# A two-layer transformer block on one core: gate and up products interleaved in the first batch's FFN, and five score banks in the last plain group

## What is computed

```
x = x + attention(norm(x))          # 16 heads of 8, softmax
x = x + ffn(norm(x))                # rounded to FP4 in blocks of 16
x = x + rotary_attention(norm(x))   # causal, own projections
x = x + mixture_of_experts(norm(x)) # top 2 of 8
# ffn: h = silu(fq(x) @ fq(w_gate).T) * (fq(x) @ fq(w_up).T); out = fq(h) @ fq(w_down).T
```

## Time and profile before

| what | us |
|---|---|
| median of 3 runs | 1920.32 (1916.94 to 1920.45) |
| the profiled execution | 1912.49 |
| its span, first to last instruction | 1910.8 |
| busy: TensorE, ScalarE, VectorE, GpSimd | 1647.2, 1442.0, 1196.8, 269.1 |

### The profile page before, as it was taken

How to read it: one execution, slowest core, us unless ns; L and a number is a source line. 1 busy time by engine, 2 the same in 40 slices (tenths; PEclk the granted TensorE clock), 3 DMA queues, 4 the chain that set the end, 5 groups by cost and what they waited for, 6 DMA issues and landing times. The chain is left out here.

```text
span 1910.8 us, 33432 instructions
## 1 busy us (share of the span) xinstructions
PE 1647.2 (86%) x12948; PEld 631.4 (33%) x12948; DVE 1196.8 (63%) x2146; ACT 1442.0 (75%) x2508; POOL 269.1 (14%) x292
## 2 busy tenths in 40 slices
PE   5599999999999999854888898998889888883995
PEld 3122222222222222242334342433333333222674
DVE  7999999999999998577364536454545423223220
ACT  4187777787877778722998999999989999992221
POOL 4400000000000000022000100010001022312466
PEclk9699999999999999966999999999999999996998
DMA  5201111111111110003111221113102222231433
GB/s 170 94 26 49 39 43 38 38 43 38 38 38 44 38 38 22 7 25 111 55 50 59 73 86 50 51 58 108 47 32 73 79 88 95 99 118 47 133 57 30
DMA packets 69839, 115.85 MB, mean 61 GB/s; under 512 B 9689, under 2 KB 54597, under 8 KB 65072
## 3 DMA queue, kind: packets, MB, share of 16 engines
q1 hardware_dynamic: 58416, 92.87, 15.3%
q0 software_dynamic: 11264, 20.83, 4.0%
HBM read 71.49 MB, written 42.14 MB: 59 GB/s over the span
## 5 line engine op out<-in xcount | busy, mean ns | idle before, releaser
L750 ACT ACTIVATE rows_and_probs<-psS 128x512 f32<-128x512 f32 x1024 | 556.4, 596 | 179.3 <-PE psS L648 177.6
L772 DVE TENSOR_REDUCE max_of_halves<-psM 128x2 f32<-128x1024 f32 x512 | 617.7, 1222 | 44.7 <-PE psM L617 15.4
L1574 ACT ACTIVATE exps<-cpsS 128x1024 bf16<-128x1024 f32 x512 | 545.6, 1107 | 25.4 <-PE cpsS L1338 24.7
L1338 PE MATMUL cpsS<-rotary_stack 128*128 128x512 bf16 x1024 | 302.9, 386 | 70.6 <-ACT exps L1574 28.7
L668 PE MATMUL psO<-rows_and_probs,plain_v 128*9 128x256 f32 x4096 | 317.1, 382 | 4.9 <-issue 2.3
L1584 ACT ACTIVATE cprobs<-cpsS 128x1024 f32<-128x1024 f32 x256 | 281.2, 1098 | 21.7 <-PE cpsO L1371 18.9
L1318 PE MATMUL cpsS<-rotary_stack 128*128 128x512 bf16 (+3 forms) x768 | 193.7, 329 | 53.5 <-ACT exps L1574 36.4
L617 PE MATMUL psM<-plain_top 64*128 64x512 bf16 x1024 | 209.8, 391 | 24.4 <-DVE max_of_halves L772 24.1
L648 PE MATMUL psS<-plain_top 64*128 64x512 bf16 x1024 | 213.2, 388 | 6.5 <-issue 6.5
L648 PE MATMUL psS<-plain_rest 64*128 64x512 bf16 x1024 | 207.7, 378 | 0.0
L1371 PE MATMUL cpsO<-cprobs,rotary_v 128*9 128x512 f32 (+3 forms) x1536 | 153.7, 488 | 0.8 <-DVE rotary_sums L1908 0.8
(11 more groups left out here) (294 smaller groups left out, 1682.4 us busy)
## 6 DMA issues: line engine op xcount, KB each, us to landing
rotary_stack<-q_parts SPq DMA_DIRECT2D x48, 192.0 KB
rotary_stack<-k_parts SPq DMA_DIRECT2D x48, 192.0 KB
rotary_stack<-q_rot_parts SPq DMA_DIRECT2D x48, 192.0 KB
rotary_stack<-k_rot_parts SPq DMA_DIRECT2D x48, 192.0 KB
tokens_taken<-parts_and_sums POOLq DMA_DIRECT2D x32, 259.0 KB, 4.2
plain_top<-q_parts SPq DMA_DIRECT2D x64, 96.0 KB
plain_top<-k_parts SPq DMA_DIRECT2D x64, 96.0 KB
e_x<-tokens_taken SPq DMA_DIRECT2D x8, 518.0 KB, 9.3
```

What stands on the lines that cost most here:

```text
L750: act.activation(pr[n % SLOTS_P][:, h, :], psS[u % RING][:, :], ACT.Exp, scale=SCALE).then_inc(s_e, 1)
L772: dve.tensor_reduce(mh[g % 2][:, :, hh, t, kh:kh + 1].rearrange("p e o -> p (e o)"), psM[n % 2][:, :, :], AX.X, ALU.max).then_inc(s_r, 1)
L1338: ins = pe.matmul(to[:, kh, :], q[:, x, y_ * P:(y_ + 1) * P], k[:, x, kh * CH:(kh + 1) * CH], start=True, stop=True)
L1574: act.activation(ex[d % EX][:, :, :], psS[n % 3][:, :, :], ACT.Exp, scale=SCALE, accum_out=den[:, at:at + 1]).then_inc(s_e, 1)
```

## The change

In the plain phase the scores of group 15 go round over five banks, the three of `psS` and the pair of `psM` that `merge_turn(15)` will use at the end. `last_user(u)` names the unit whose exponential frees the bank. Units 3 and 4 of the group instead wait for VectorE to have read the last turn out of that pair.

In the late phase VectorE clears the corners first, in the order of banks 4, 5, 6, 0, 1, 2, 3, and `cpsO` last. TensorE begins with the gate weights after the first clear, then turns the up and down weights, each after its bank's clear. The projection weights become a task of their own, `wq`, behind the last up product, with a bank of the ring. ScalarE copies the gate and up weights first, the down weights ahead of the first tanh, and the projection weights at `wq`. TensorE waits for two copies before the first gates, for four before the up products and later gates, for twelve before the projections. A gate needs the up product of the tile before. By the planner's rule, which I worked through, the order becomes

```diff
@@ -600,6 +600,19 @@
+        LAST, spare = (G - 1) * UNITS, psM[use["merge", G - 1, 0] % 2]
+        last_banks = [psS[(LAST + i) % RING][:, :] for i in range(RING)] + [spare[:, i, :] for i in range(2)]
+        def score_bank(u):
+            return psS[u % RING][:, :] if u < LAST else last_banks[(u - LAST) % len(last_banks)]
+        def last_user(u):
+            if u >= LAST + len(last_banks):
+                return u - len(last_banks)
+            return u - RING if RING <= u < LAST + RING else None
@@ -642,10 +655,15 @@
                         u, h = u0 + n, HEADS[i + n]
-                        if part == 0 and u >= RING:
-                            pe.wait_ge(s_e, u - RING + 1)
+                        if part == 0:
+                            before = last_user(u)
+                            if before is None and u >= RING:
+                                pe.wait_ge(s_r, use["turn", G - 1, 0] + 1)
+                            elif before is not None:
+                                pe.wait_ge(s_e, before + 1)
                         rows, hh = rows_of(h // (HG // 2)), h % (HG // 2)
-                        ins = pe.matmul(psS[u % RING][:, :], k[rows, hh, j * P:(j + 1) * P],
+                        ins = pe.matmul(score_bank(u), k[rows, hh, j * P:(j + 1) * P],
                                         q[rows, hh, cq * CH:(cq + 1) * CH], start=(part == 0), stop=(part == 1),
@@ -747,7 +765,7 @@
                         act.wait_ge(s_s, u + 1)
-                        act.activation(pr[n % SLOTS_P][:, h, :], psS[u % RING][:, :], ACT.Exp,
+                        act.activation(pr[n % SLOTS_P][:, h, :], score_bank(u), ACT.Exp,
                                        scale=SCALE).then_inc(s_e, 1)
@@ -1018,7 +1036,7 @@
     for t in range(TB):
-        tasks.append((("g", n, t), "slot", 0.5, [("x", n, t // TC)], 0.0))
+        tasks.append((("g", n, t), "slot", 0.5, [("x", n, t // TC)] + ([("u", n, t - 1)] if t and n == 0 else []), 0.0))
     if n:
@@ -1031,9 +1049,11 @@
                 tasks.append((("round_h", n, t // 2), "vector", 7.0, [("u", n, t), ("u", n, t - 1)], 0.0))
+    if n == 0:
+        tasks.append((("wq", n), "slot", 2.0, [("u", n, TB - 1)], 0.0))
     for c in range(2):
         for t in range(c * TC, (c + 1) * TC):
-            tasks.append((("h", n, t), "slot", 0.55, [("round_h", n, t // 2), ("d", n, c - 1)], 0.0))
+            tasks.append((("h", n, t), "slot", 0.55, [("round_h", n, t // 2), ("d", n, c - 1)] + ([("u", n, TB - 1)] if n == 0 else []), 0.0))
         tasks.append((("d", n, c), "slot", 0.7, [("h", n, t) for t in range(c * TC, (c + 1) * TC)], 0.0))
@@ -1160,7 +1180,7 @@
-    SLOT_KINDS = ("x", "g", "u", "h", "d", "px", "a", "s", "v", "m", "fy", "fo", "rt", "l", "ps")
+    SLOT_KINDS = ("wq", "x", "g", "u", "h", "d", "px", "a", "s", "v", "m", "fy", "fo", "rt", "l", "ps")
     use, bank_of, earlier = {}, [], []
@@ -1175,7 +1195,7 @@
     for label, k in use.items():
-        act_keeps = label[1] == 0 and label[0] in ("x", "h", "px")
+        act_keeps = label[1] == 0 and label[0] in ("x", "h", "px", "wq")
         if act_keeps:
@@ -1259,7 +1279,7 @@
         block = c.enter_context(nc.Block())
-        KEPT = 12
+        UP_KEPT, DOWN_KEPT, KEPT = 2, 4, 12
         BLOCKS = 2 * I // QB
@@ -1375,6 +1395,8 @@
                     wait_kept(pe, ("h", n, cc * TC + i))
+                    if n == 0:
+                        pe.wait_ge(s_wk, DOWN_KEPT)
                     for j, (at, width) in enumerate(FC):
@@ -1400,8 +1422,14 @@
                         ins = pe.transpose(to[:, i * P:(i + 1) * P], rows, p.ident[:, :])
+                elif kind == "wq":
+                    pe.wait_ge(s_w, 16 * 5)
+                    for t in range(4):
+                        ins = pe.transpose(to[:, t * P:(t + 1) * P], raw[:, t, :], p.ident[:, :])
                 elif kind in ("g", "u"):
                     t = label[2]
+                    if n == 0:
+                        pe.wait_ge(s_wk, UP_KEPT if (kind, t) < ("g", TC) else DOWN_KEPT)
                     wait_kept(pe, ("x", n, t // TC))
@@ -1417,10 +1445,14 @@
                     wait_kept(pe, ("px", n, cc))
+                    if n == 0:
+                        pe.wait_ge(s_wk, KEPT)
                     ins = pe.matmul(to[:, :], w[:, k if kind == "a" else 3 + k, :], xt[:, cc * CH:(cc + 1) * CH],
...
                     wait_kept(pe, ("px", n, label[2]))
+                    if n == 0:
+                        pe.wait_ge(s_wk, KEPT)
                     for i in range(TC):
@@ -1451,21 +1483,21 @@
-            pe.wait_ge(s_oz, 1 + len(banks))
             pe.wait_ge(fw.s_wq, 2)
+            for k in range(2):
+                pe.wait_ge(s_oz, k + 1)
+                for j, (at, width) in enumerate(FC):
+                    ins = pe.transpose(banks[4 + k][:, at:at + width], fw.raw[0:width, 3 * k + j, :], p.ident[0:width, 0:width])
+                ins.then_inc(s_wt, 1)
             for j, (at, width) in enumerate(FC):
-                ins = pe.transpose(banks[1][0:width, j * P:(j + 1) * P], fw.rawd[:, at:at + width], p.ident[:, :])
+                pe.wait_ge(s_oz, 3)
+                ins = pe.transpose(banks[6][0:width, j * P:(j + 1) * P], fw.rawd[:, at:at + width], p.ident[:, :])
             ins.then_inc(s_wt, 1)
-            for k in range(2):
-                for j, (at, width) in enumerate(FC):
-                    ins = pe.transpose(banks[2 + k][:, at:at + width], fw.raw[0:width, 3 * k + j, :], p.ident[0:width, 0:width])
-                ins.then_inc(s_wt, 1)
-            pe.wait_ge(s_w, 16 * 5)
-            for t in range(4):
-                ins = pe.transpose(banks[4][:, t * P:(t + 1) * P], raw[:, t, :], p.ident[:, :])
-            ins.then_inc(s_wt, 1)
-            pe.wait_ge(s_wk, KEPT)
             for _, label in plans[0]:
+                if label[0] == "x":
+                    pe.wait_ge(s_oz, 4 + label[2])
+                elif label == ("g", 0, 0):
+                    pe.wait_ge(s_oz, len(banks) + 1)
                 fill(label)
@@ -1494,24 +1526,29 @@
             def keep_weights():
-                act.wait_ge(s_wt, 1)
-                act.activation(wd[:, 0:2, :], banks[1][:, 0:2 * P].rearrange("p (c d) -> p c d", c=2), ACT.Copy).then_inc(s_wk, 1)
+                for k in range(2):
+                    act.wait_ge(s_wt, k + 1)
+                    act.activation(wg[:, k, :], banks[4 + k][:, 0:I], ACT.Copy).then_inc(s_wk, 1)
+            def keep_down():
+                turned = banks[6]
+                act.wait_ge(s_wt, 3)
+                act.activation(wd[:, 0:2, :], turned[:, 0:2 * P].rearrange("p (c d) -> p c d", c=2), ACT.Copy).then_inc(s_wk, 1)
                 last = FC[2][1]
-                act.activation(wd[0:last, 2, :], banks[1][0:last, 2 * P:3 * P], ACT.Copy).then_inc(s_wk, 1)
+                act.activation(wd[0:last, 2, :], turned[0:last, 2 * P:3 * P], ACT.Copy).then_inc(s_wk, 1)
+            def keep_square(turned):
                 for k in range(2):
-                    act.wait_ge(s_wt, k + 2)
-                    act.activation(wg[:, k, :], banks[2 + k][:, 0:I], ACT.Copy).then_inc(s_wk, 1)
-                act.wait_ge(s_wt, 4)
-                for k in range(2):
-                    src = banks[4][:, k * D:(k + 1) * D]
+                    src = turned[:, k * D:(k + 1) * D]
                     act.activation(w[:, k, :].rearrange("p (a d h) -> p a d h", a=HG, d=DH),
...
                         act.activation(to[:, i, :, :, :], src[:, 1 - i, :, :, :], ACT.Copy).then_inc(s_wk, 1)
-                act.activation(w[:, 2, :], banks[4][:, 2 * D:3 * D], ACT.Copy).then_inc(s_wk, 1)
-                act.activation(wo[:, :], banks[4][:, 3 * D:4 * D], ACT.Copy).then_inc(s_wk, 1)
+                act.activation(w[:, 2, :], turned[:, 2 * D:3 * D], ACT.Copy).then_inc(s_wk, 1)
+                act.activation(wo[:, :], turned[:, 3 * D:4 * D], ACT.Copy).then_inc(s_wk, 1)
+                act.wait_ge(s_wk, KEPT)
@@ -1529,6 +1566,8 @@
                 elif kind == "g" and n == 0:
+                    if label[2] == 0:
+                        keep_down()
                     act.wait_ge(s_f, use[label] + 1)
@@ -1549,7 +1588,10 @@
                     act.wait_ge(s_f, use[label] + 1)
-                    if kind in ("x", "px"):
+                    if kind == "wq":
+                        keep_square(bank(label))
+                        act.sem_inc(s_ka, 1)
+                    elif kind in ("x", "px"):
                         cc = label[2]
@@ -1722,7 +1764,7 @@
                 elif half == 0:
-                    dve.wait_ge(s_wt, 4)
+                    wait_read(dve, ("wq", 0))
                 mine = slice(half * TC * HG, (half + 1) * TC * HG)
@@ -1907,10 +1949,9 @@
+            for to in banks[4:] + banks[:4]:
+                dve.memset(to[FC[2][1]:P, 2 * P:3 * P], 0.0).then_inc(s_oz, 1)
             dve.memset(psO[:, :], 0.0).then_inc(s_oz, 1)
-            for to in banks:
```

(1 more changed line is left out.)

## The result

| | before | after |
|---|---|---|
| median of 5 runs, us | 1917.0 (1915.71 to 1920.45) | 1903.76 (1901.3 to 1907.75) |
| ratio, 95% interval | | 0.9928 [0.9917, 0.9939] |
| span of the profiled execution | 1910.8 | 1900.5 |

The change is faster, by 13.2 us between the medians.

A forecast was written before the change was run, and what follows sets the result against it. It took a loop of exponentials, value sums and scores to bound the last plain group, VectorE the stage to 903, ScalarE the rotary phase. Gains 0.3 + 9.9 = 10.2 us from 1920.32 gave 1910.1 us, range 1904.5 to 1916.

The forecast's parts named there:

- Five banks: Last plain group: scores wait for the exponential five before, not three; 0.3 us gained, bounds 0 and 3.2.
- no link of it waits for a bank: Last plain group: the 2.38 us loop of exponentials, value sums and scores never waits for a bank, so it stays.
- Rival A: Last plain group: TensorE, no longer late, also shortens waits for each half's first scores, up to 3.2 us; 1907.2, chance 0.10.
- Start of TensorE: Head of the late phase: one small clear precedes TensorE instead of 1.60 us of clears, so it starts at 810.13.
- First scaling: Head of the late phase: VectorE's first scaling at 819.2 instead of 829.07, 9.9 us earlier (9.4 to 10.8).
- Rounds: Rounding: two gates more per round are free, 7.10 us against 7.11; three rounds change by 0 (-0.2 to +1.9).
- Rival B: Rounding: GpSimd holds the second gate, 1912.0, chance 0.07; or holds all four products, 1921.5, chance 0.04.
- Projection weights: Late phase: their transposes and ScalarE's copies, moved behind the last up product, cost 0; without cover 2.5 us.
- Rival E: Head: planner doesn't interleave as the diff says, or last weight load is still awaited in front; 1918.6, chance 0.03.
- Second down product: Behind the last rounding: unchanged, 0 taken; wholly full clock would give 1.35 us, wholly half would cost 0.9.
- rival C: Before 903: down product becomes the bound, or stores fall due in another order; half the gain, 1915, chance 0.06.
- rival D: Rotary phase: its 16 groups lose their rhythm and ScalarE stands longer; 1926 at 1 us a group, chance 0.05.

The follow-up runs named there:

- late_only: The changed kernel with three score banks in the last plain group, as before the change; 1906.48 us, ratio 0.9942 to the kernel before.
- four_banks: The changed kernel with four score banks in the last plain group instead of five; 1902.43 us (2 runs), ratio 0.9933 to the kernel before.
- again: The changed kernel, unedited, run once more on another chip; 1903.06 us, ratio 0.9937 to the kernel before.
- unedited_beside: The changed kernel, unedited, run once more beside two other versions on the same chip; 1903.44 us, ratio 0.9937 to the kernel before.
- projections_in_front: The changed kernel with projection weights turned ahead of the rows, down-weight copies in front and all twelve copies awaited; 1914.6 us, 0.9983 to the kernel before.
- gates_first: The changed kernel without a gate's need for the preceding up product, so eight gates come first; 1909.78 us, ratio 0.9951 to the kernel before.
- four_scores: The changed kernel, issuing all four scores of a half before the previous half's value sums in the last plain group; 1899.86 us, 0.9921 to the kernel before.
- plain_only: The kernel before with only the five score banks in the last plain group; 1917.99 us, ratio 0.9996 to the kernel before.

## Why the prediction was wrong, point by point

Three terms were too small: the banks by 0.5 us, the first scaling by 1.3, the second down product by 1.35. The sign, the order of the terms and the mechanism of the largest were right. In the profiled executions group and head gave 13.8 us against 10.2 in the sum; the three terms are 3.2 of the difference, and 0.5 lie in small ones behind them. Behind the second and the third term stands one omission: TensorE's clock was put at a value between its two levels where the execution was at the full one. Between the medians the change gave 13.2, so the sum was 3.0 us short, and it was taken from a median that was itself 3.3 us too high. Together these are the 6.3 us between 1910.1 and 1903.76.

- **The median it was taken from** (1920.32, three runs between 1916.94 and 1920.45). Two more runs brought it to 1917.0, and other chips gave 1918.39, 1914.39 and 1915.42. I had written that a median scatters by some 2 us; the three runs were 3.3 off. The profiled execution, at 1912.49, had pointed the other way, and the forecast gave it no weight.
- **Five banks: 0.3 taken, 0.83 measured.** The step that failed is "no link of it waits for a bank". One did, in front of the value sums. In the kernel before they start 0.31 us behind the start of the last second part in front of them, also where they have waited for exponentials: those at 791.55 stand 0.31 behind a second part of 791.25, and 0.10 behind the end of the exponential they wait for. That second part was late because its score had waited for a bank. In the changed kernel the waiting sums of 792.48 start 0.46 us behind the last second part (792.02) and 0.05 behind the end of the exponential (792.43), which alone holds them now. So a half takes 2.33 us instead of 2.38, and 0.05 in each of sixteen halves is 0.8. `late_only`, on three banks, has the 0.31 and the 0.10 again, and `four_banks` shows that a fifth bank is without effect. Rival A was right that there was more, but the 3.2 us of its end did not come.
- **Start of TensorE: right.** 6.66 us after the last plain exponential, 1.42 earlier (forecast 811.56 - 810.13 = 1.43).
- **First scaling: 9.9 taken, 11.2 measured** (10.8 in `again`, 11.0 in `unedited_beside`), beyond the end of 10.8 that was given for "all at full". Three steps were too slow, each by 0.4 or 0.5 us. "Nine transposes at 0.21 apart" gave 1.92 us until the rows are turned; it was 1.45 (810.73 to 812.18), since the clock was still granted in full until 811.2 (in `again` 1.84). "The old distance holds" from rows turned to the first gate gave 3.97; it was 3.58 (812.18 to 815.76; `again` 3.60): TensorE had been at work since 810.73, and the clock rose at 814.6, while the first products ran. In `late_only`, where it rose only at 816.5, the distance was 3.96 as before. And "I take 819.2" put 3.2 us between first gate and first scaling, between 3.6 for the half clock and 2.3 for the full one; at the full one it took 2.69 (815.76 to 818.45), so that bound was itself 0.4 too low. That TensorE now works earlier and that the clock rises after such work was argued in the text, and then not used.
- **ScalarE's copies of the down weights: right.** They ended at 815.16, forecast 815.2.
- **Rounds: right.** 0 forecast; rounds of 7.13 and 7.12 us, tiny operations of 0.34 and 0.96 against 0.4 and 0.96. Rival B is excluded: the gate at 823.47 lies wholly beside GpSimd's operation of 822.43 to 824.10 and takes 0.51 us, its usual length. By the rule of the Trainium skill, "SBUF — State Buffer", section "Who interferes with whom", it should, and the trace agrees. The other half of the argument, that GpSimd is what they hide behind, is shown by the pair without it.
- **Projection weights: right, cost 0.** Turned at 831.45, forecast 831.3; the first down product ended at 843.00 and VectorE wanted it at 846.36, 3.4 us of slack where I gave 2.3. Rival E is excluded by `projections_in_front`.
- **Second down product: 0 taken, 1.35 measured.** The bound was in the text ("wholly at the full clock this would give 1.35 back"): the addition follows the first one's by 4.42 us instead of 5.77 in all four profiles of the changed kernel with four or five banks (4.41 to 4.42), and `gates_first` (6.67) has the other bound. I took a value between two levels as the likeliest, though the executions are at one level or the other or pass from one to the other within the product. Why the changed kernel finds the full clock there so often is not shown; `late_only` (5.22) and `four_scores` (5.49), which differ from it in the plain group alone, don't.
- **"Moves rigidly" up to 903:** nearly. The stretch from the first rotation to the bias took 20.73 and 20.75 us (20.91 before), but 22.89 in `unedited_beside`: the half clock falls there instead. This is the weak form of rival C, worth 2.2 us in some executions, and it lies inside the difference between 0.9928 and 0.9937.
- **Rotary phase, rival D:** excluded. From the first start to the last, its exponentials took 825.2 to 826.9 us in the four profiles of the changed kernel with four or five banks, before 825.17. `plain_only`, whose head is that of before, has the longest of all runs, 827.5, so these 2 us of scatter don't follow from the earlier start of the phase.

What put the result outside the range is the start. The lower end allowed the 13.4 us of gain of rival A and 2 us of scatter, which from 1920.32 is 1904.9 (the text has 1904.5); from 1917.0 the same terms would have reached 1901.6. The terms themselves were too narrow as well: with 12.5 us as the most that the forecast's own case allowed, the 13.2 measured lie beyond it. Two more of its numbers don't come out exactly: the upper end by the terms named is 1917.3 and not 1916, and the second case of rival B 1921.8 and not 1921.5. Neither bears on the result.

## What to carry to other kernels

Give an engine the work whose result is wanted late exactly where it already stands for another engine, and price that by the other engine's period, not by the length of the work: here six gates were free, and without GpSimd they cost 0.78 us more than they gave. A load that is waited for costs what stands behind it in the queue; moving the weights that need it behind the urgent work brought three times what the order of gates and up products did (8.58 against 2.79 us at the addition of the first down product). And where an engine waits after each round of a loop, look at what is queued between the wait and the work that the other engine needs: putting four scores in front of the value sums took 5.6 us out of a stretch of 39 in which five banks had found 0.8.

## What had not been expected of the hardware

- A value sum starts at the earliest 0.31 us behind the start of the second part of the last score in front of it (0.46 where it waits for an exponential longer than that); a delay of one of the two scores that start together can therefore delay the loop, though the other is in time.
- Exponentials of 128x512 are recorded as 0.60 us each, or up to 0.7 where they follow without a gap (`four_scores`), and start 0.49 us apart when nothing is awaited (three in 1.48 us).
- The same kernel, on the same data, has its half clock at different places: 24 passes of the down product took 2.84 us at the full clock and 5.03 almost wholly at the half one (in `gates_first`), the eight passes of the value products 1.13 to 1.92. Which of them pays differs between executions, by up to 2.2 us.
